# Where a hybrid state-space and mixture-of-experts kernel keeps its intermediate rows, logits and output stage

## What is computed

```
xn   = x * rsqrt(mean(x*x)) * norm_w;  xb, gate = split(xn @ W_in.T)
xc   = silu(causal_conv4(xb) + conv_b)
dt   = soft_clamp(softplus(xc @ W_dt.T + b_dt), 0.001, 0.1)
h    = h * exp(soft_clamp(dt*A)) + dt*B*xc      # every 10th step: h *= min(20/|h|, 1)
y    = sum_n(h * C) + D * xc
x2   = layernorm(2*x + s * (y * silu(gate)) @ W_out.T)
top2 experts of softmax(x2 @ w_router); position in the expert by a running count,
tokens at or above 768 are dropped; expert: relu(t @ w1 + b1) @ w2 + b2
out  = layernorm(x2 + sum of the two gated expert outputs)
```

## Time and profile before

| | us |
|---|---|
| median of 3 runs | 3176.89 (3172.8 to 3178.94) |
| the profiled execution, its own time | 3173.14 |
| its span, first to last instruction | 3171.3 |

### The profile page before, as it was taken

One profiled execution on the slowest core, in us unless ns is written; L12 is line 12 of the kernel. 1 busy time (PEld: TensorE's weight loads), 2 busy tenths in 40 slices (PEclk: granted clock), 3 DMA queues, 4 the chain that ended last, 5 costly groups with the idle time before them and its releaser, 6 DMA issues. The chain is left out here.

```text
span 3171.3 us, 50661 instructions
## 1 busy us (share of the span) xinstructions
PE 2664.3 (84%) x16400; PEld 2425.7 (76%) x16400; DVE 2591.2 (82%) x3910; ACT 2262.9 (71%) x5130; POOL 1987.0 (63%) x1978
## 2 busy tenths in 40 slices
PE   3699989989989989989889989998998873799980
PEld 3688888888888888888888888888888763666760
DVE  1699999999999999999999999999999977212115
ACT  2888888888888888888888888888888820111114
POOL 1477777777777777777677777777777751333322
PEclk9899999999999999999999999999999886899995
DMA  3122122122222222222222222221222212433317
GB/s 153 57 63 67 59 70 68 64 70 68 63 71 66 64 69 65 66 69 66 63 70 63 67 71 62 69 68 60 72 70 62 66 40 73 131 75 90 83 19 240
DMA packets 173256, 234.03 MB, mean 74 GB/s; under 512 B 51776, under 2 KB 115008, under 8 KB 172608
## 3 DMA queue, kind: packets, MB, share of 16 engines
q1 hardware_dynamic: 149232, 197.48, 20.3%
q0 software_dynamic: 9216, 12.59, 2.2%
q10 hardware_dynamic: 14544, 20.74, 1.9%
HBM read 197.65 MB, written 33.05 MB: 73 GB/s over the span
## 5 line engine op out<-in xcount | busy, mean ns | idle before, releaser
L627 POOL TENSOR_TENSOR H<-H,CB 128x640 f32<-128x640 f32 x832 | 1242.0, 1493 | 500.0 <-DVE H L466 496.9
L466 DVE TENSOR_TENSOR_SCAN H<-DA,PM 128x704 f32<-128x704 f32 x832 | 1321.9, 1605 | 2.8 <-ACT DA L266 2.1
L372 ACT ACTIVATE DA<-DT,AS 128x160 f32<-128x160 f32 x3328 | 1106.1, 425 | 1.3
L649 PE MATMUL YB<-H,ID 128*128 128x160 f32 x6656 | 1051.8, 310 | 0.5 <-POOL H L627 0.5
L649 PEld LDWEIGHTS YB<-H,ID 128*128 128x128 f32 x6656 | 991.0, 192 | 16.7 <-issue 11.2
L439 DVE TENSOR_TENSOR PM<-PM,BB 128x640 f32<-128x640 f32 x832 | 640.5, 814 | 4.7
L266 ACT ACTIVATE DA<-DA 128x2560 f32<-128x2560 f32 x208 | 484.6, 2330 | 1.6
L674 PE MATMUL PA<-XC,WDT 128*128 128x160 f32 x832 | 170.1, 373 | 146.8 <-DVE XC L515 146.8
L674 PEld LDWEIGHTS PA<-XC,WDT 128*128 128x128 f32 x832 | 157.0, 248 | 162.4 <-DVE XC L515 162.4
L618 POOL TENSOR_TENSOR FC<-SN,HALF 128x4 f32<-128x4 f32 x206 | 210.5, 1022 | 94.6 <-DVE SN L472 90.6
L454 DVE TENSOR_SCALAR PM<-H,FC 128x64 f32<-128x64 f32 x824 | 229.1, 322 | 0.0
(11 more groups left out here) (165 smaller groups left out, 3674.6 us busy)
## 6 DMA issues: line engine op xcount, KB each, us to landing
BB<-Bd SPq DMA_DIRECT2D x208, 320.0 KB, 3.4
CB<-Cd SPq DMA_DIRECT2D x208, 320.0 KB, 3.2
W<-in_w ACTq DMA_DIRECT2D x16, 1024.0 KB, 7.8
XT<-in_xT SPq DMA_DIRECT2D x52, 160.0 KB, 2.2
XR<-in_xp SPq DMA_DIRECT2D x416, 20.0 KB
X2d<-VV SPq DMA_DIRECT2D x416, 20.0 KB
HI<-X2d SPq DMA_DIRECT2D x8, 1024.0 KB, 11.2
HT<-YA SPq DMA_DIRECT2D x8, 1024.0 KB, 8.5
```

The lines of the kernel that those rows point to most:

```text
L372: eng.activation(DA[:, c0:c0 + 2, :, a, m, 1:11].rearrange("p c b t -> p b c t"), DT[:, j % 2, a].rearrange("p b (c t) -> p b c t", c=2), ...
L466: eng.tensor_tensor_scan(H[:, q % 3, u], a0, DBX(u), 0.0, ALU.mult, ALU.add).then_inc(s_scan, 1)
L627: eng.tensor_tensor(h, h, cb, ALU.mult).then_inc(s_hc, 1)
L649: mm = eng.matmul(yv, ID[:], hv[:, :, :, n, 0:10], start=False, stop=n == 15)
```

## The change

- Nothing is written to `YA` ahead of the loop and `H` isn't set to zero. SP stores each chunk of x2 twice instead, to `X2d` and to `YA`: 16 DMAs in slot 2, where there were 8. DVE waits for both before it overwrites `VV`. The experts' outputs are then added to x2 in `YA`.
- The small constants are one packed tensor `SM`; SP loads it, the first `XT` and the identity, ACT the five weight tensors. The preparations are split: ACT and PE start after ten of them, POOL after 28, the first projection after 30, and the rest is awaited just ahead of chunk 0.
- `LGd` has the router's layout, [128, 64, 8]. A store of 20 tokens is cut in two where it crosses a multiple of 128 tokens (7 chunks of the 52); the last chunk's stores are issued by ACT. The router loads `LG` with one DMA in rows of 2 KB, and its constants with one DMA (`MC`) on ACT's queue; the first reduction waits for `LG` alone.
- In the router, the triangular matrix has 1 taken off each element, so that the scan runs straight on PSUM, with no copy and no subtraction; the gate work stands beside the matmuls; the steps for both choices are one instruction of twice the size.
- The lane numbers are copied to PSUM and the indicators read them there. DVE makes only indicators. ACT makes the row products of n = 0 (16 instructions of 128x48 for each chunk), POOL the row products of n = 1 and the gates of both.
- The last stage fetches `YA` alone, 8 KB for each partition (token = 8p + j), into eight buffers, so that no fetch waits for a buffer. DVE only computes statistics; POOL makes 1/sqrt with `pow` and scales 3 of 8 pieces, ACT the other 5. Each sequence is written with two DMAs of 5 KB and 3 KB rows.

The core of the diff:

```
-            rows = H[:].rearrange("p a b c -> p (a b c)")
-            yr = YA.rearrange("(p r) n -> p (r n)", p=128)
-            eng.wait_ge(s_h0, 1)
-            for f, n in ((0, 33 * 256), (33 * 256, 32 * 256)):
-                eng.dma_start(yr[:, f:f + n], rows[:, 0:n]).then_inc(s_ya0, 16)
+            eng.dma_start(SM[:], d["small"]).then_inc(s_small, 16)
+            eng.dma_start(XT[:, 0], d["xT"][0]).then_inc(s_xt[0], 16)
+            eng.dma_start(ID[:], d["ident"]).then_inc(s_small, 16)
...
+        def lg_out(eng, j):
+            eng.wait_ge(s_lgs, j + 1)
+            for g in range(2):
+                for b in range(4):
+                    for l, h, r in parts(j):
+                        eng.dma_start(LGd[l % 128:l % 128 + h - l, 8 * (4 * g + b) + l // 128, :],
+                                      LGS[20 * b + r:20 * b + r + h - l, g, :]).then_inc(s_lgd, 16)
...
                         eng.wait_ge(s_x2, 2 * (j + 1))
+                        for to, done in ((X2d, s_x2d), (YA, s_ya)):
+                            for g in range(2):
+                                for b in range(4):
+                                    r0 = LP * (4 * g + b) + T * j
+                                    eng.dma_start(to[r0:r0 + T, :], VV[20 * b:20 * b + 20, g, :]).then_inc(done, 16)
...
                             eng.wait_ge(s_x2d, 128 * j)
+                            eng.wait_ge(s_ya, 128 * j)
...
+            eng.dma_start(LG[:], LGd).then_inc(s_lg, 16)
...
+            for b in range(B):
+                eng.dma_start(rows(b), YB[b, 10:10 + L, :].rearrange("(p j) n -> p j n", p=128)).then_inc(s_xf[b], 16)
+            for b in range(B):
+                o = out[L * b:L * b + L, :].rearrange("(p j) n -> p j n", p=128)
+                for j0, j1, done, n in ((0, 5, s_x3a, 5), (5, 8, s_x3p, 3)):
+                    eng.wait_ge(done, n * (b + 1))
+                    eng.dma_start(o[:, j0:j1], rows(b)[:, j0:j1]).then_inc(s_out, 16)
...
+                for n in (1, 0):
+                    eng.wait_ge(s_row[n], c + 1 if n else 16 * (c + 1))
+                    eng.tensor_tensor(HI[:, n, j, 48:96], HI[:, n, j, 48:96],
+                                      GA[:, n, j].unsqueeze(2).to_broadcast([128, 16, 48]), ALU.mult).then_inc(s_gate[n], 1)
...
+                eng.wait_ge(s_mv, 8 * (b + 1))
+                eng.tensor_scalar(SD[:, b], MV[:, b % 4, :, 1], 1.0, 1e-5, ALU.mult, ALU.add).then_inc(s_va, 1)
+                eng.tensor_scalar(NM[:, b], MV[:, b % 4, :, 0], -1.0, 0.0, ALU.mult, ALU.add).then_inc(s_va, 1)
+                eng.wait_ge(s_va, 3 * b + 2)
+                eng.tensor_tensor(SD[:, b], SD[:, b], HALF[:], ALU.pow).then_inc(s_va, 1)
+                eng.wait_ge(s_va, 3 * b + 3)
+                eng.tensor_tensor(NM[:, b], NM[:, b], SD[:, b], ALU.mult).then_inc(s_nm, 1)
+                eng.wait_ge(s_nm, b + 1)
+                for j in range(5, 8):
+                    eng.tensor_scalar(x[:, j], x[:, j], SD[:, b, j:j + 1], NM[:, b, j:j + 1],
+                                      ALU.mult, ALU.add).then_inc(s_x3p, 1)
```

More of the change, by code:

```diff
@@ L184, in sync_program @@
                     q = 4 * i + r
-                    if s == 0 and ok(i + 4):
+                    if s == 0 and ok(i + 4) and i + 4 > 0:
                         j = i + 4
@@ L207, in sync_program @@
                                       ).then_inc(s_cb[p % 2], 16)
[L208 to L214, removed]
+                    if s == 1 and ok(i - 3) and i - 3 < NB - 1:
+                        lg_out(eng, i - 3)
                     if s == 2 and ok(i - 2):
@@ L840, in moe_phase @@
         s_yo = [sem(f"yo{n}") for n in range(3)]
-        s_xf = [sem("xf0"), sem("xf1")]
-        s_yf = [sem(f"yf{n}") for n in range(3)]
-        s_sum = [sem("sum0"), sem("sum1")]
-        s_bn, s_mv, s_sd, s_rc, s_x3 = sem("bn"), sem("mv"), sem("sd"), sem("rc"), sem("x3")
-        s_out = [sem(f"out{n}") for n in range(6)]
-        RT_P, RT_MM, RT_CN, RT_G, RT_IX = 6, 21, 22, 51, 56
-        LD_ALL = 16 * 13
-        XRW = X2d.rearrange("b r n -> (b r) n")
+        s_xf = [sem(f"xf{n}") for n in range(B)]
+        s_bn, s_mv, s_va, s_nm, s_x3a, s_x3p, s_out = (
+            sem("bn"), sem("mv"), sem("va"), sem("nm"), sem("x3a"), sem("x3p"), sem("out"))
+        RT_P, RT_MM, RT_G, RT_IX = 6, 21, 37, 42
+        XRW = X2d
         XF = HI[:].rearrange("p a b c -> p (a b c)").rearrange("p (k j n) -> p k j n", k=6, j=8)
@@ L854, in moe_phase, with rows @@
         GP = PB[1][:, 0:96]
+        IOP = PB[7][:, 0:128]
+        def rows(b):
+            return XF[:, b] if b < 6 else YF[:, b - 6]
         def bank(n):
@@ L931, in scalar_program @@
             load_w(1)
+            eng.wait_ge(s_rt, RT_G)
+            for c in range(4):
+                eng.wait_ge(s_eq[0], c + 1)
+                for j in range(16 * c, 16 * c + 16):
+                    eng.activation(HI[:, 0, j, 0:48], HI[:, 0, j, 48:96], ACT.Copy,
+                                   scale=TK[:, j:j + 1]).then_inc(s_row[0], 1)
             eng.wait_ge(s_bl, 32)
@@ L1118, in gpsimd_program @@
+            for b in range(B):
+                x = rows(b)
+                eng.wait_ge(s_xf[b], 16)
+                if b >= 4:
+                    eng.wait_ge(s_nm, b - 3)
+                for j in range(8):
+                    eng.bn_stats(BN[:, b % 4, j], x[:, j]).then_inc(s_bn, 1)
+                eng.wait_ge(s_bn, 8 * (b + 1))
+                for j in range(8):
+                    eng.bn_aggr(MV[:, b % 4, j], BN[:, b % 4, j]).then_inc(s_mv, 1)
         def gpsimd_program(eng):
             eng.wait_ge(s_rt, RT_G)
+            eng.wait_ge(s_ld, 16)
@@ L1163, in tensor_program @@
         def tensor_program(eng):
             eng.wait_ge(s_rt, RT_MM)
[L1165 to L1167 removed]
+            eng.wait_ge(s_ld, 16)
+            mm = MM[:].rearrange("p e j -> p (e j)")
+            eng.matmul(PB[0][:], TRI, mm, start=True, stop=True).then_inc(s_rp, 1)
             eng.matmul(PB[1][:], ONE[:], mm, start=True, stop=True).then_inc(s_rp, 1)
[L1169 removed]
+            eng.wait_ge(s_rt, RT_G)
@@ L1170, in tensor_program @@
             for c in range(4):
-                for n in range(2):
-                    eng.wait_ge(s_hi[n], 2 * (c + 1))
-                    eng.wait_ge(s_lo, 2 * c + n + 1)
+                for n in (1, 0):
+                    eng.wait_ge(s_lo, 2 * c + 2 - n)
+                    eng.wait_ge(s_gate[n], c + 1)
                     for j in range(16):
-                        t = eng.matmul(GP, LO[:, c % 2, n, j], HI[:, n, 16 * c + j], start=(c, n, j) == (0, 0, 0),
-                                       stop=(c, n, j) == (3, 1, 15))
+                        t = eng.matmul(GP, LO[:, c % 2, n, j], HI[:, n, 16 * c + j], start=(c, n, j) == (0, 1, 0),
+                                       stop=(c, n, j) == (3, 0, 15))
@@ L1257 @@
     wbc[:, 32:48] = a["L0_attn_W_C"].T
+    small = np.zeros((128, 96), np.float32)
+    small[:, 0:64] = a["L0_attn_A_log"].reshape(4, 128, 16).transpose(1, 0, 2).reshape(128, 64)
+    small[:, 64:80] = a["L0_attn_conv_w"].reshape(4, 128, 4).transpose(1, 0, 2).reshape(128, 16)
+    for k, n in enumerate(("L0_attn_conv_b", "L0_attn_b_dt", "L0_attn_D_param")):
+        small[:, 80 + 4 * k:84 + 4 * k] = a[n].reshape(4, 128).T
+    small[:, 92:94] = a["L0_attn_norm_w"].reshape(2, 128).T
+    small[:, 94] = a["L0_attn_residual_scale"].reshape(-1)[0]
     arrays = {
```

343 lines of the change are left out of this document (126 added, 217 removed).

## The result

The changed kernel takes 3087.03 us (median of four runs, 3084.8 to 3090.23), the kernel before 3174.96 (3172.8 to 3178.94) beside it: a ratio of 0.9722, with a 95% interval from 0.9708 to 0.9737. Its profiled execution has an own time of 3084.80 us and a span of 3082.6, which is 88.7 less than before.

What follows compares the result with a forecast made beforehand. DVE bounds the loop (96% busy), PE's pace the experts; start, router and last stage are chains with idle engines. Gains sum to 87.2 us: span 3084.1, own time 3085.9, plus 3.75 gives 3090 us, range 3076 to 3105.

Steps and rivals of the forecast that it cites:

- Start: Kernel start: without the zero write the first projection comes at 14.4 us in place of 45.61, gain 31.2 us.
- Rival (e): Kernel start: the weights, not the zeros, hold it; projection at 20 us, 3096 us in all; chance 0.05.
- Loop: Steady loop: extra wait and stores cost 0, bounds -5 and +6 us; last stores end 0.3 us later.
- The cover of 5.4 us: Loop, SP's queue: BB lands at 1514.4, DVE first reads it at 1519.77, leaving 5.4 us where there were 9.1.
- Router: Router chain after the softmax: 12.1 us of 30 instructions become 7.2, gain 4.9 us (4 to 5.5).
- Lists: Building the lists: PE becomes the bound, 37.2 us in place of 47.2, gain 9.9 us.
- (b): Lists: PE stays at the low clock, 1.6 us lost in place of 9.9 gained; 3102 us; chance 0.08.
- (c): Lists: DVE and POOL hold each other up, a chunk takes 12.7 us; 3108 us in all; chance 0.05.
- Gathers: First gathers after the lists: the sixth takes 3.4 us in place of 5.93, gain 2.5 us (0.5 to 3.2).
- Last stage: Output stage: transfers at 380 GB/s and POOL at 4.4 us a sequence end about together, at 3141.5; gain 29.8 us.
- Rival (a): Last stage gives less: stores queue behind fetches, or POOL needs 5.6 us a sequence; 3102 us; chance 0.14.
- (d): Loop: SP's extra store issues make BB late; at 1.5 us an issue 148 us lost, 3238 us; chance 0.03.

## Where the prediction was right and where it was off

The forecast was 3090, the median is 3087.03. Own time was put at 3085.9 and is 3084.80. The median lies 2.2 us above it, not the 3.75 of the kernel before, which I had carried over: half of the small miss is that. The stages miss in both directions, 3.9 us of more gain and 2.4 of less, so that the sum is off by 1.5 is in part luck.

*Start: 31.2 predicted, 29.98 measured.* The step that was off by 1.2 is when ACT's queue is free. I let its five issues end at 4.95, as before; the fifth, `WR`, now takes 3.05 us in place of 1.90, they end at 6.13, and the table load at 7.44. Then ACT waits 0.26 more for the identity. The 7.4 us from Square to projection held (7.38). Rival (e) didn't come: the weights were scaled by 13.3.

*Loop: -0.3 predicted, -0.50 measured.* The trips are as long as before and DVE never waits for `BB` or for the stores. The cover of 5.4 us was the right quantity: 16 issues more, 6.6 us, made it give way. The last stores delayed the end by 1.0 rather than 0.3; the loop itself gave 0.5.

*Logits: 9.2 against 9.08.* The landing took 3.5, put at 3.2.

*Router: 4.9 predicted, 5.3 measured net.* Two errors. The small instructions of 128 elements start 0.13 us after each other where none waits for the one before; I had 0.3. Against that, `MM` written in another layout takes 1.03 in place of 0.69, and the two matmuls with the wait for them 3.82 in place of 3.55, which I had not costed: the 0.60 ahead of the scan.

*Lists: 9.9 predicted, 12.05 measured, the largest miss.* The term that was mis-sized is the time at the low clock. I took 50 records at 0.171, then full clock. There were 59 records in 8.56 us, 0.145 each: the granted clock was 0.76 in that stretch, where the earlier trace rows have 0.63. That is 1.0 us of the miss. PE could start 4.3 us in, not 4.9, because POOL's product took 1.48 and not 1.9: 0.6. The later records took 0.113 and not 0.115: 0.4. Rivals (b) and (c) didn't come, but what each is about is there in a smaller size. Hold-ups between DVE and POOL, (c), cost 9 us as soon as the lane numbers stay in SBUF; half of the 18 that I priced, as a chunk then takes 9.98 and not 12.7. The low clock, (b), lasted for the first 4 us or so and cost 2.0.

*Gathers: 2.5 against 3.15*; the sixth took 2.8 us, not 3.4. The first expert took 22.84 in place of 23.50, for nothing that I had counted.

*Last stage: 29.8 against 28.97.* The sum came near in part by luck. POOL's 4.4 a sequence was 4.34 and pow on 8 elements 1.65, as its slope over two rows said. The end came 5.7 us after POOL's and not 3.3: ACT ends 0.9 behind POOL, and issue and landing of the last stores take 4.8, with 2.9 for a landing in the earlier trace rows; the 0.8 that I had added for two limits at one place covered part of this. Transfers were put at 380 GB/s and ran at 428 in and 414 out, so the second limit was slack, and I called two limits equal of which one bound. The Trainium skill's page "DMA: Bandwidth & Descriptors", section "Bandwidth", has both figures: about 358 GB/s as HBM's limit for one core, and 425 for a 16 MB load issued from GpSimd with the pair's other core idle. The 428 here, with fetches alone, go with the second.

Rival (a) didn't come, nor (d); (d) takes 32 stores to begin.

Not taken apart by a run, only read in the two traces, are the gains at the logits and the gathers, and how the last stage's gain is shared between half the fetch traffic, the eight buffers and the additions that are gone.

## What to carry to other kernels

Read a start, a router and an output stage as chains, and ask of each for the wait that ends last: 68 of the 88.7 us came from stages in which engines had been idle for loads, stores and buffers, and none from the loop that fills four fifths of the time. Before two SBUF operands go to DVE beside a busy GpSimd, move the constant one to PSUM, and before an instruction is moved, look at what the other engine does at its new place. When an engine is relieved, work out what is next: here one edit in the split of 5 to 3 was worth 5.3 us, and 8 KB rows 1.0 us before it was made and 5.6 after.

## What the runs showed of the hardware

- Rows of 1 KB moved 348 GB/s into SBUF and 385 out of it; rows of 8 KB moved 428 in, and rows of 5 and 3 KB 414 out. Six issues of 1 MB in a row took SP 2.94 us with 8 KB rows and 12.02 with 1 KB rows; of those the first two took 0.39 and 0.57 and the fourth 3.47, so this isn't the price of an issue alone.
- A product of two SBUF tensors on DVE that starts in the midst of a GpSimd product that reads SBUF ends 0.34 to 0.36 us after it, whatever is left of that (45 of 45): 1.15 and 1.51 us in place of 0.49 in the rows above. It stands in the trace as busy time of DVE.
- GpSimd's pow grows by 0.16 us with each element of a partition, on top of some 0.38: 0.702 us for 2, 1.022 for 4, 1.65 for 8.
- In the first 8.6 us of the lists PE's granted clock was 0.76 behind a pause of 10.58 us and behind one of 4.82 (a mean over a part at 1.2 and a part at 2.4 GHz), and 1.00 behind one of 0.61. Of the 2.0 us won in the lists by the full clock, 0.9 were lost in the first expert's first layer.
